# First attention of a two-layer block: score tiles and their maxima two heads at a time, turned tiles and exponentials one head at a time, the score mask added in the maximum

## The reference

```python
h = layernorm(x, ln1_g, ln1_b)
qkv = (h @ Wqkv).reshape(Bb, Tt, H, 3 * hd)
q, k, v = (qkv[..., :hd], qkv[..., hd:2 * hd], qkv[..., 2 * hd:])
q, k = (rope(q), rope(k))
scores = jnp.einsum('bqhd,bkhd->bhqk', q, k) / math.sqrt(hd)
causal = jnp.tril(jnp.ones((Tt, Tt), dtype=bool))
scores = jnp.where(causal, scores, jnp.asarray(-1000000000.0, scores.dtype))
probs = jax.nn.softmax(scores, axis=-1)
attn = jnp.einsum('bhqk,bkhd->bqhd', probs, v).reshape(Bb, Tt, d) @ Wproj
x = x + attn
```

## Time and profile before

| | |
|---|---|
| three runs | 3013.8, 3019.21, 3020.83 us; median 3019.21 us |
| profiled execution, first to last instruction | 3006.4 us (12.8 below the median of the runs) |
| busy share of that span | PE 94%, PEld 44%, DVE 67%, ACT 51%, POOL 33% |
| mean granted TensorE clock | 0.969 of full speed |
| the stage of the change | from 259.7 to 1083.6 us, 823.9 us |

### The profile page before, as it was taken

One profiled execution on the slowest core, in us unless ns is written; L12 is line 12 of the kernel. 1 busy time (PEld: TensorE's weight loads), 2 busy tenths in 40 slices (PEclk: granted clock), 3 DMA queues, 4 the chain that ended last, 5 costly groups with the idle time before them and its releaser, 6 DMA issues. The chain is left out here.

```text
span 3006.4 us, 46248 instructions
## 1 busy us (share of the span) xinstructions
PE 2831.9 (94%) x18017; PEld 1317.3 (44%) x18017; DVE 2010.2 (67%) x4329; ACT 1545.3 (51%) x2581; POOL 990.0 (33%) x533
## 2 busy tenths in 40 slices
PE   7998999999999976999999899899999999999999
PEld 4664233333333344666676545323333333333327
DVE  7887899999999845000000565688787877878823
ACT  3452477676777755222222444345565665565571
POOL 1000000110101103111101330157777777777791
PEclk9997899999999987999999999889999999999999
DMA  4322122133202124232111466312020220202103
GB/s 130 97 77 76 37 51 39 43 62 66 50 24 62 24 68 130 63 86 75 63 48 34 148 193 185 79 32 61 8 64 12 68 64 8 64 12 68 67 12 119
DMA packets 141306, 200.77 MB, mean 67 GB/s; under 512 B 14320, under 2 KB 107904, under 8 KB 138000
## 3 DMA queue, kind: packets, MB, share of 16 engines
q1 hardware_dynamic: 130672, 173.21, 20.9%
q0 software_dynamic: 9056, 24.59, 3.9%
q10 hardware_dynamic: 1360, 0.01, 0.0%
HBM read 121.21 MB, written 76.02 MB: 66 GB/s over the span
## 5 line engine op out<-in xcount | busy, mean ns | idle before, releaser
L946 ACT ACTIVATE at_probs<-at_st 128x512 f32<-128x512 f32 (+3 forms) x1280 | 588.5, 542 | 442.1 <-PE at_st L1040 282.4
L909 POOL TENSOR_TENSOR at_probs<-at_probs 128x2048 f32<-128x2048 f32 (+3 forms) x205 | 725.9, 3546 | 214.7 <-ACT at_probs L946 135.4
L393 DVE TENSOR_REDUCE at_part<-at_s 128x1 f32<-128x512 f32 (+3 forms) x1280 | 690.0, 603 | 63.0 <-PE at_s L431 28.6
L368 ACT ACTIVATE at_probs<-at_st 128x1024 f32<-128x1024 f32 (+3 forms) x640 | 541.6, 895 | 275.4 <-PE at_st L450 141.0
L972 DVE TENSOR_REDUCE at_part<-at_s 128x1 f32<-128x512 f32 x768 | 498.5, 683 | 67.8 <-PE at_s L1032 63.9
L966 DVE CUSTOM_DVE_ANT_0 at_s<-at_s,at_later 128x384 f32<-128x384 f32 (+3 forms) x512 | 246.9, 498 | 103.8 <-PE at_s L1032 102.4
L510 PE MATMUL at_acc<-at_probs,at_v 128*32 128x512 f32 (+3 forms) x2560 | 305.5, 551 | 8.2 <-ACT at_otile L355 7.8
L2358 DVE TENSOR_TENSOR ex_ot<-ex_bank,lin_b 128x512 f32<-128x512 f32 x32 | 22.2, 692 | 426.3 <-PE ex_bank L2388 352.2
L2321 ACT ACTIVATE ex_hT<-ex_bank,ex_b 128x512 f32<-128x512 f32 x128 | 87.9, 687 | 334.7 <-PE ex_bank L2378 332.7
L2378 PE MATMUL ex_bank<-ex_xT,lin_w 128*128 128x512 f32 x512 | 225.5, 598 | 1.0 <-ACT ex_xT L2314 1.0
L2388 PE MATMUL ex_bank<-lin_w,ex_hT 128*128 128x256 f32 x1024 | 223.7, 379 | 0.8 <-ACT ex_hT L2321 0.8
(11 more groups left out here) (342 smaller groups left out, 3950.0 us busy)
## 6 DMA issues: line engine op xcount, KB each, us to landing
att<-at_otile SPq DMA_DIRECT2D x64, 256.0 KB, 2.1
lin_w<-in_W SPq DMA_DIRECT2D x16, 1024.0 KB, 7.5
at_v<-v SPq DMA_DIRECT2D x11, 1024.0 KB, 11.1
v<-pr_vt SPq DMA_DIRECT2D x32, 256.0 KB
exp_out<-ex_ot SPq DMA_DIRECT2D x32, 256.0 KB, 2.1
v<-p_vt SPq DMA_DIRECT2D x32, 256.0 KB, 3.7
p_xs<-in_x SPq DMA_DIRECT2D x8, 512.0 KB, 5.2
qhi<-p_parts SPq DMA_DIRECT2D x8, 512.0 KB
```

Source lines behind the costliest of these rows:

```text
L368: act.activation(probs[:, quad % RING, heads_down * p:heads_down * (p + 1), off:QB], st_ps[n % st_slots][:, :, off:QB], ACT.Exp, scale=EXP ...
L393: dve.tensor_reduce(part[:, w % 2, qt * HG + h, j:j + 1], s_ps[n % S_SLOTS][:, 0:width], AX.X, ALU.max).then_inc(item_free, 1)
L909: pool.tensor_tensor(total, total, probs[:, slots.slot[quad], :, off:QB], ALU.add).then_inc(add_done, 1)
L946: act.activation(probs[:, slots.slot[quad], h, off:QB], st_ps[n % ST_SLOTS][:, off:QB], ACT.Exp, scale=EXP_SCALE).then_inc(exp_done, 1)
```

## The change

- A score item is now two heads: two banks, two matmuls side by side (L456), 640 items in 2 slots. DVE takes both maxima in one `tensor_reduce` with two results (L423).
- On the diagonal the two mask matmuls of a head go. DVE adds the mask while it takes the maximum: `tensor_tensor_reduce`, one for each head, with the table `later` in SBUF (L419). It writes the sum back in place.
- A turned item is now one head: one bank, one activation of up to 512 elements (L389), 1280 items in 3 slots.
- The copy of the turned maxima out of PSUM moves from DVE to ACT (L377), and the empty DVE instruction behind it goes. TensorE waits for a slot by what the item in it was (`freed`).
- The planner gets costs for this, and so the order changes. SP's store of a unit and DVE's reciprocal keep their distance (4 and 30 items of two heads are now 8 and 60 of one). One table less is made for the masks, an unused one goes from the constants (`mask_qk`), and POOL makes `later` once.

```diff
 def narrow_schedule():
-    heads_down, st_slots, s_slots = 2, 2, 3
-    parts = HG // heads_down
+    heads_down, st_slots, s_slots = 2, 3, 2
...
-                        n += 1
-                        if late and n == 4:
-                            ahead.append(("T", late))
-                            late = None
+                    ahead.append(("S", unit, qt, h0, j, QB if j < u else (qt + 1) * P))
+                    n += 1
+                    if late and n == 2:
+                        ahead.append(("T", late))
+                        late = None
         ahead.append(("M", unit))
...
             else:
                 of_unit = of_unit + 1 if of_unit < count[ev[1]] else 1
-                end = start + ev[5] * COLUMN + (110 if ev[4] == ev[1][1] else 0)
-                issue, rows[ev[3] % heads_down] = start + 30, end
-                pe = max(pe, end)
-                dve = max(dve + ev[5] * 1.04 + 25, end + 220 + ev[5] * 1.04 + 125)
-            slot_free[n_item % s_slots] = dve
+                pe = issue = start + ev[5] * COLUMN + 30
+                rows = [pe] * heads_down
+                dve = max(dve - 60, pe + 220) + heads_down * ev[5] * 1.04 + (190 if ev[4] == ev[1][1] else 125)
+                slot_free[n_item % s_slots] = dve
...
             body.append(("ST",) + s + (part,))
             mode = 16
-            pe = start + w * COLUMN + (110 if diagonal2(s) else 0)
...
-            act = max(act + heads_down * w * 0.833 + 95, max(pe + 220, needs) + heads_down * w * 0.833 + 185)
+            act = max(act + w * 0.833 + 67, max(rows[part % heads_down] + 220, needs) + w * 0.833 + 185)
             st_free[n_pair % st_slots] = act
...
     def make(self, pool):
-        for wide in self.tiles:
-            pool.memset(wide[:, :], 0.0).then_inc(self.cleared, 1)
+        for tile in (*self.tiles, self.later):
+            pool.memset(tile[:, :], 0.0).then_inc(self.cleared, 1)
         pool.wait_ge(self.cleared, 3)
+        last = self.later[:, QB - P:QB]
+        pool.affine_select(out=last, in_=last, compare_op=ALU.is_ge, fill=MASK, base=0, pattern=[[-1, P]],
+                           channel_multiplier=1).then_inc(self.ready, 1)
...
+                if ev[0] == "T":
+                    t = place_of[ev[1]]
+                    act.wait_ge(item_ready, item + 1)
+                    if t >= 2:
+                        act.wait_ge(row_ready[t % 2], 16 * HG * (t // 2))
+                    act.activation(strip[:, t % 2, :], s_ps[item % S_SLOTS][0:2 * HG, 0, 0:QB // 2].bitcast(F16),
+                                   ACT.Copy).then_inc(strip_ready, 1)
+                if ev[0] in ("S", "T"):
+                    item += 1
...
-                act.activation(probs[:, quad % RING, heads_down * p:heads_down * (p + 1), off:QB],
-                               st_ps[n % st_slots][:, :, off:QB],
+                act.activation(probs[:, quad % RING, h, off:QB], st_ps[n % st_slots][:, off:QB],
                                ACT.Exp, scale=EXP_SCALE).then_inc(exp_done, 1)
...
+                    place = s_ps[n % S_SLOTS][:, :, 0:width]
+                    to = part[:, w % 2, qt * HG + h:qt * HG + h + heads_down, j]
                     dve.wait_ge(item_ready, n + 1)
-                    dve.tensor_reduce(part[:, w % 2, qt * HG + h, j:j + 1],
-                                      s_ps[n % S_SLOTS][:, 0:width], AX.X, ALU.max).then_inc(item_free, 1)
+                    if j == u:
+                        for y in range(heads_down):
+                            dve.tensor_tensor_reduce(out=place[:, y], in0=place[:, y], in1=masks.later[:, QB - width:QB],
+                                                     scale=1.0, scalar=MASK, op0=ALU.add, op1=ALU.max,
+                                                     accum_out=to[:, y:y + 1]).then_inc(item_reduced, 1)
+                        reduced += heads_down
+                    else:
+                        dve.tensor_reduce(to, place, AX.X, ALU.max).then_inc(item_reduced, 1)
+                        reduced += 1
...
-                    t = place_of[ev[1]]
-                    dve.wait_ge(item_ready, n + 1)
-                    if t >= 2:
-                        dve.wait_ge(row_ready[t % 2], 16 * HG * (t // 2))
-                    dve.tensor_copy(strip[:, t % 2, :], s_ps[n % S_SLOTS][0:2 * HG, 0:QB // 2].bitcast(F16)
-                                    ).then_inc(strip_ready, 1)
-                    dve.wait_ge(strip_ready, t + 1)
-                    dve.nop().then_inc(item_free, 1)
...
+            def take(n):
+                if n >= S_SLOTS:
+                    by, count = freed[n - S_SLOTS]
+                    pe.wait_ge(free_sem[by], count)
...
+                take(n)
+                for y in range(heads_down):
+                    rows = slice(base(y), base(y) + K)
+                    mm = pe.matmul(s_ps[n % S_SLOTS][:, y, 0:width], QT[g % 2][rows, h0 // heads_down, q0:q0 + P],
+                                   KT[g % 2][rows, h0 // heads_down, j * QB:j * QB + width], start=True, stop=True)
                 mm.then_inc(item_ready, 1)
...
                 place = st_ps[n % st_slots]
-                heads = range(heads_down * p, heads_down * (p + 1))
-                for y, h in enumerate(heads):
-                    rows = slice(base(h), base(h) + K + 2)
-                    mm = pe.matmul(place[:, y, off:QB], KT[g % 2][rows, h // heads_down, kc * P:(kc + 1) * P],
-                                   QT[g % 2][rows, h // heads_down, u * QB + off:(u + 1) * QB],
-                                   start=True, stop=not diagonal)
+                rows = slice(base(h), base(h) + K + 2)
+                mm = pe.matmul(place[:, off:QB], KT[g % 2][rows, h // heads_down, kc * P:(kc + 1) * P],
+                               QT[g % 2][rows, h // heads_down, u * QB + off:(u + 1) * QB],
+                               start=True, stop=not diagonal)
```

More of the change, by code:

```diff
@@ L127, in narrow_schedule @@
                     ready = max(ready, pv_end[last_of[g - 2]] + 12000)
-                row = max(issue, rows[ev[3] % heads_down]) if ev[0] == "S" else pe
-                start = max(row, ready) + turn(16)
+                start = max(pe, ready) + turn(16)
                 choice.append((start - 100 + (500 if lead() > 3 else 0), 0, "S", start))
@@ L133, in narrow_schedule @@
             if s[0] in row_at and n_pair // parts - n_quad < RING:
-                start = max(pe, st_free[n_pair % st_slots] + 60, row_at[s[0]]) + turn(16)
+                start = max(issue, rows[part % heads_down], st_free[n_pair % st_slots] + 60, row_at[s[0]]) + turn(16)
                 choice.append((start, 1, "ST", start))
@@ L172, in narrow_schedule @@
             mode = 16
-            pe = start + w * COLUMN + (110 if diagonal2(s) else 0)
-            issue, rows = pe - w * COLUMN, [pe] * heads_down
+            issue, rows[part % heads_down] = start + 30, start + w * COLUMN + (150 if diagonal2(s) else 0)
+            pe = max(pe, rows[part % heads_down])
             quad = n_pair // parts
@@ L247, in narrow_attention @@
     last_unit = {g: [x for x in units if x[0] == g][-1] for g in range(GROUPS)}
-    LATER = 30
+    freed, reduced = [], 0
+    for ev in body:
+        if ev[0] == "T":
+            freed.append(("strip", place_of[ev[1]] + 1))
+        elif ev[0] == "S":
+            reduced += heads_down if ev[4] == ev[1][1] else 1
+            freed.append(("reduced", reduced))
+    LATER = 60
     QK_LOADS = 6 * heads_down * 16
@@ L260, in narrow_attention @@
         otile = c.sb("otile", [P, 2, QB], F32)
-        ident_wide, mask_wide, back_wide = masks.tiles
-        st_ps = [c.ps(f"st{k}", [P, heads_down, QB]) for k in range(st_slots)]
-        s_ps = [c.ps(f"s{k}", [P, QB]) for k in range(S_SLOTS)]
+        ident_wide, back_wide = masks.tiles
+        st_ps = [c.ps(f"st{k}", [P, QB]) for k in range(st_slots)]
+        s_ps = [c.ps(f"s{k}", [P, heads_down, QB]) for k in range(S_SLOTS)]
         acc_ps = c.ps("acc", [P, QB])
@@ L355, in evict @@
                 act.activation(otile[:, evicted % 2, :], acc_ps[:, :], ACT.Copy).then_inc(out_ready, 1)
+            item = 0
             for ev in body:
@@ L380, in _ @@
         def _(dve):
-            n, w = 0, 0
+            n, w, reduced = 0, 0, 0
             due = []
+            dve.wait_ge(masks.ready, 5)
             for ev in body:
@@ L446, in key_tile @@
                 place = st_ps[n % st_slots]
[L447 to L452 removed]
+                rows = slice(base(h), base(h) + K + 2)
+                mm = pe.matmul(place[:, off:QB], KT[g % 2][rows, h // heads_down, kc * P:(kc + 1) * P],
+                               QT[g % 2][rows, h // heads_down, u * QB + off:(u + 1) * QB],
+                               start=True, stop=not diagonal)
                 if diagonal:
                     for half in range(2):
[L455 to L459 removed]
+                        rows = slice(base(h), base(h) + 64)
```

(4 more changed lines are left out.)

77 lines of the change are left out of this document (29 added, 48 removed).

## The result

The changed kernel takes 3033.0 us (median of four runs, 3032.4 to 3035.6), the kernel before 3017.0 (four runs, 3013.8 to 3020.8). The ratio is 1.0060, 95% interval 1.0046 to 1.0074: slower by 0.6%, 16 us, where the forecast was 3004 and faster. The time lies in the range of 2963 to 3041. Its quads without a score item do cost DVE time, as the runs show too.

The account below looks back on a forecast made before the run. The prediction took DVE, with its 1280 maxima, to set the pace for 781.6 us. Its terms -25 + 17 - 18 + 16 - 20 + 9 + 6 = -15 us gave 3004 us, in a range of 2963 to 3041.

Parts of the forecast that it names:

- Maxima off the diagonal: DVE's maxima on 768 tiles off the diagonal: 384 two-head reductions each save 0.065 us fixed cost, 25 us less.
- Masked maxima: 512 diagonal maxima on DVE, now with the mask added: 5 us plus 12 us, together 17 us more.
- Copies of T: 32 copies of the turned maxima out of PSUM leave DVE for ACT, 0.55 us each: 18 us less.
- The slot of T: The score slot holding turned maxima waits for ACT's copy: 0.5 us of stand for each of 32, 16 us more.
- DVE's stands: DVE's waits for TensorE's score tiles: with mask matmuls gone, more items are ready in time, 20 of 51.8 us go.
- The uneven order: 32 of the first 290 quads have no score item, 3 before: 0.3 us for each of 29, 9 us more.
- second rival: Slower: 1.3 us for each of 29 quads without score item, 0.8 us per turned-maxima copy; 3035 us, chance 0.31.
- ACT and the end: Behind the last score item 28.5 quads instead of 20: 48 us for 42.3, so 6 us more; ACT otherwise hidden.
- The Trainium skill's figures: Fixed costs from PSUM: 125 ns per DVE instruction (48 us saved by merging, not 25), 143 ns per ScalarE instruction (forecast 3010).

Follow-up runs that it names:

- t_dve: The changed kernel with the copy of the turned maxima back on DVE, order untouched; ratio 1.0063 to the kernel before.
- pair_pe: The changed kernel, order untouched, with masks back on TensorE, all 640 score items reduced two heads at a time, turned maxima copied on DVE; 1.0033 of the kernel before.
- after_end7: The changed kernel, same order, but behind the last copy of turned maxima the turned items use seven slots instead of three; 1.0037 of the kernel before.
- st3: The kernel before with turned items of one head in 3 slots, one bank unused, order planned anew; ratio 1.0163 to the kernel before.
- st4: The kernel before with turned items of one head in 4 slots of one bank, order planned anew; ratio 0.9998 to the kernel before.
- st2: The changed kernel with two slots for turned items instead of three, one bank unused, order planned anew; ratio 1.0846 to the kernel before.

## Why the prediction was wrong

- **Maxima off the diagonal**, -25: right, 27 by the rows. All 640 merged give 46.6 (73 ns each).
- **Masked maxima**, +17: near. 22 alone; in pairs t_dve has 35.8 more than pair_pe, of which about 19 (256 x 73 ns) is merging not done, which leaves 17.
- **Copies of T**, -18: too large. 10 us of busy time went. The 0.55 from start to next start also held 0.14 in which DVE stood, as the copy itself took 0.41.
- **The slot of T**, +16: right, 12.6 and 15.5.
- **DVE's stands**, -20: this step failed. Without T's 12.6 the stands went from 62.5 to 71.1, +9, where -20 and +9 (the uneven order) were forecast, -11 together. The prediction said that "more score items are ready in time" since TensorE loses work. It priced slots for T and for DVE, but not the third slot of the turned items. TensorE's list is in order, so a stand for an exponential also holds the score items behind it: 42.3 us of DVE's stands come behind a stand of TensorE at a turned item, 33.9 of them behind one that an exponential ended.
- **The uneven order**, +9: too small. 23.6 us of DVE's stands end at the first score item behind a stretch without any, 0.8 us for each of the 29 quads more: more than the 0.3 of the forecast, less than the 1.3 of the second rival, and about at the price from which that rival was to decide. 23.3 of them also come behind a stand for a fourth head. The two can't be parted here: such a quad takes 2.39 us because of its slots, and two full slots feed DVE for 2.26.
- **ACT and the end**, +6: this step failed as well. 45 us for the quads was counted from ACT's exponentials, 2.0 us a quad; three slots made it 2.39. Measured 63.5 for 48. With seven slots 55.1: 8.4 us are the slots, and 7 more than forecast are left even then.

The terms to the last maximum were to give -21 and gave 0; the end was to give +6 and gave +21. Both misses have a root in common, the missing slot. after_end7 shows it at the end, with the order unchanged: 8.4 us. Before the last maximum it is shown by st3 against st4 only together with the order. The second root is the order, with 8.5 more quads at the end and 32 without score items. How the rest divides between the two was not measured. The kernels hold a sign that the prediction does not use: `narrow_schedule` also returns where its own clock of TensorE ends, 765.9 us for the kernel before and 816.5 for the changed one (779.0 for st4, 812.6 for st3, 945.5 for st2). It put the changed kernel 51 us behind, which is too much (its costs are not those of the rows) but on the right side.

Two sums of the prediction do not come out. The second rival's terms, +24 and +44, give 3043 and 3063 and not 3035, and lie above the range's 3041. And 5 us more by the figure for exponentials make 3009 and not 3010. The Trainium skill's figures weighed in the prediction ("VectorE: DVE Perf Modes", section on the TRN2 errata) do not fit: merging saved 73 ns an instruction and not 125, and in the changed kernel four exponentials of one head take 2.06 us where two of two heads took 1.94, 60 ns for each one more and not 143.

## What to carry to other kernels

When banks (parts of PSUM) are handed from one stream of tiles to another, write out the ring that each stream runs with its new slot count: what the in-order engine issues, in which place it first waits, and what is queued behind. Work taken off the busiest engine comes back only if the engine that feeds it is not made to wait for a third one. And look at what is behind the last item of the bounding engine: an order that moves work there is paid in full. Where the order comes from a planner with a clock of its own, compare what that clock says of both orders before the run.

## What the runs showed of the hardware

Taking small matmuls away from TensorE made the kernel slower. With the same DVE work, 1024 matmuls of 128 columns against zeros hold S at 801.1 us, and without them it is 813.3, the mean clock 0.95 and 0.90. The medians are 3017.9 and 3032.2 us, and the intervals of their ratios do not overlap. The same removal inside the changed kernel shows no such fall (t_dve against pair_pe: 71 and 67 us at the lower level in S), so it isn't the matmuls alone; what else it takes was not taken further. The end of st2, where TensorE stands twice a quad, had a mean clock of 0.54: 117 of its 127.3 us at 0.5 of full speed. There a sum of full width takes 1.93 us (at 1242.05) for 1.06 at full speed.
